# Three short token tiles at the end of each expert layer

## The chip, the cores and the metric

The kernel runs on one core of one Trainium2 chip. The time is device microseconds of one execution; a result is the median over runs. All transfers between HBM and the core's memory go over 16 DMA engines. Engines are named as in the profile: PE is TensorE (PEld its weight loads), DVE is VectorE, ACT is ScalarE, POOL is GpSimd, SP is SyncE. A name with a q behind it (SPq, ACTq) is that engine's queue issuing a transfer.

## The reference

A small vision network on 16 images of 32 x 32 positions with 96 channels, float32: 16,384 tokens. Two blocks follow each other. Each has a mixer over the image (the first with attention along rows and columns, the second a convolution and a state-space scan) and then a layer of experts, each part added to its input:

```python
x = x + mixer0(ln_c(x))
t = t + experts0(ln_t(t))      # t: x as 16384 tokens of 96
x = x + mixer1(ln_c(x))
t = t + experts1(ln_t(t))

def experts(x, gate_w, gate_b, w1, b1, w2, b2):
    scores = einsum('bsd,de->bse', x, gate_w) + gate_b
    probs = softmax(scores)                      # 4 experts
    masked = probs * (probs is among the top 2)
    masked = masked / (sum(masked) + 1e-9)
    h = gelu(einsum('bsd,edh->ebsh', x, w1) + b1)      # 96 -> 384
    y = einsum('ebsh,ehd->ebsd', h, w2) + b2           # 384 -> 96
    return einsum('bse,ebsd->bsd', masked, y)
```

## The kernel before

The program is written by hand, engine by engine: each engine has its own instruction order, and semaphores join them. Nothing is reordered by a scheduler. The stages follow each other: mixer 0, expert layer 0, mixer 1, expert layer 1.

**Routing.** A token goes to a pair of the 4 experts, so there are `NPAIR` = 6 lists. At the end of a mixer each token's row (`ROW` = 104 numbers: 96 values, two gate weights, mean, 1/deviation, token number) is written by GpSimd's indirect DMAs (L585 in layer 0, L699 in layer 1) into its pair's region of the tensor `rows`. Then VectorE runs `planned` (from L1693): from the six counts it works out how many tiles of 512 each list has, and for each of the 37 tile places where its rows start and which two experts it needs. SyncE reads the plan: `pads` (from L481) writes 512 empty rows behind each list (L486), waits for all row scatters, and then loads tile by tile (`tokens`, L502). The number of places is fixed, `TILES` = 37, what the worst split of 16,384 tokens over six lists needs. With the reference's inputs the lists fill 34 places in layer 0 and 35 in layer 1; the places that are left, the last ones, run on empty rows, with every instruction that a full tile has, and the scatter of an empty row writes nothing, since its token number lies outside.

**One tile.** `CPT` = 6 steps c = 0 to 5, three hidden chunks of 128 for each of the two experts. A float32 product is three matmuls (`product`, L1069 to L1071) over rounded high parts and low rests. In step c of tile t:

- TensorE: `up` (3 matmuls, 128 hidden units by 512 tokens into a PSUM bank), then `down` of four steps earlier (`LAG` = 4; 3 matmuls, 96 by 512), in step 2 the transposes of the next tile's tokens (L1081), in steps 2 and 5 the transposes `y_rows` of a finished expert's output (L1109).
- ScalarE: GELU twice (L841 rounded, L842 full), in step 3 the copy of the next tile's tokens, in step 1 the bias of the first expert's output (L808). In steps 2 and 5 it asks for the weights of the next tile (L818): 673 KB for one expert, into one of two buffers, after the output of tile t-1 that used the buffer.
- VectorE: the low rest of the hidden values (L1878) in steps 0, 1, 3, 4; the bias of the second expert (L1849); `combine` (L1857), four additions for each expert; and the normalised tokens of tile t+2 (L1838).
- GpSimd: the low rest in steps 2 and 5 (L605, `ON_POOL`), and behind each of these two of the four scatters of tile t-2 (L596): each is an indirect DMA of 128 rows into the layer's output. Behind the last tile stand the scatters that are left.

A `down` waits for the low rest of its chunk, a GELU for the low rest of three steps before (`HIDS` = 3).

**Between the stages.** After expert layer 0 SyncE waits for all scatters and loads the new `x` (L546). VectorE goes on, behind its last `combine`, with the preparation of mixer 1's weights (L1265 to L1607) and then the first statistics (L1422). After layer 1 the kernel ends with the last scatters.

## Time and profile before

| | us |
|---|---|
| runs shown | 2108.26, 2111.30, 2111.42 |
| median | 2111.3 |
| the profiled execution, own time | 2104.41 |
| its span, first to last instruction | 2102.4 |
| TensorE busy | 1792.5 (85%) |
| VectorE busy | 1574.6 (75%) |
| GpSimd busy | 1288.6 (61%) |
| ScalarE busy | 1127.7 (54%) |
| DMA, mean over the span | 83 GB/s |

Expert layer 0 lies at about 369 to 745 us, expert layer 1 at about 1726 us to the end. A row of a timeline has the start, the duration, the engine, the line of the program, the operation, output<-input, the count, and in brackets how long the engine was idle before it and what released it. Matmuls are pipelined, so two that follow each other overlap in the rows; the time of one is read from start to start. The granted clock (PEclk) is TensorE's, as a share of full speed.

### The profile page before, as it was taken

What the parts mean: (1) busy time and instruction counts of PE and PEld (TensorE: products, weight loads), DVE (VectorE), ACT (ScalarE), POOL (GpSimd) and SP (SyncE); (2) the same over time, 40 slices, a digit from 0 to 9 for tenths busy, and PEclk for the clock granted to TensorE, in tenths of its full rate; (3) what the DMA queues carried; (4) which work ended last, traced back from release to release, by engine and by line L of the source; (5) the groups of instructions that cost most, each with busy time, mean ns of one, the idle gap of its engine ahead of it and who ended that gap; (6) DMA issues with size and microseconds to landing.
All of it is one profiled execution on the core that took longest, in us unless ns stands there. A gap on an engine that the chain in (4) does not pass through costs nothing.

```text
span 2102.4 us, 65544 instructions
## 1 busy us (share of the span) xinstructions
PE 1792.5 (85%) x25858; PEld 1433.2 (68%) x25858; DVE 1574.6 (75%) x5089; ACT 1127.7 (54%) x2201; POOL 1288.6 (61%) x1350
## 2 busy tenths in 40 slices
PE   4877830899999939999999999999999809999997
PEld 2766630677777737887777777777878607777775
DVE  6688761677777657888989898988888737777775
ACT  2434200677777745555555545545544207777775
POOL 3347757378877734545466756556666565776776
PEclk9776665899999969999999999998999559999998
DMA  9310103465555470000000000000000034555553
GB/s 150 90 58 30 33 31 139 134 198 184 183 193 187 141 121 3 3 3 3 4 10 12 11 10 12 9 11 10 12 11 12 16 129 143 189 184 189 184 189 98
DMA packets 95797, 174.94 MB, mean 83 GB/s; under 512 B 53618, under 2 KB 66955, under 8 KB 95492
## 3 DMA queue, kind: packets, MB, share of 16 engines
q10 hardware_dynamic: 21312, 102.00, 14.6%
q1 hardware_dynamic: 56516, 42.48, 8.8%
q0 software_dynamic: 17664, 26.27, 3.7%
q8 instruction: 206, 3.38, 0.7%
q14 instruction: 99, 0.81, 0.1%
HBM read 135.33 MB, written 37.31 MB: 82 GB/s over the span
## 4 chain that ended last, share of the span: by engine, by line
PE 56%; DVE 22%; issue 8%; POOL 6%; ACT 5%; DMA 2%; SPq 0%; DVEq 0%; ACTq 0%; POOLq 0%
PE ps L1069 10%; PE ps L1070 9%; PE ps L1071 9%; PE ps L1150 6%; POOL rows L585 4%; PE ps L1185 3%; PE ps L1199 2%; PE ps L1109 2%; PE ps L1037 2%; ACT rounded L862 2%; PE ps L1081 2%; PE ps L1221 1%; DMA rounded<-weights_by_expert 1%; PE ps L1196 1%; PE ps L1040 1%
## 5 line engine op out<-in xcount | busy, mean ns | idle before, releaser
L1069 PE MATMUL ps<-rounded 97*128 97x512 f32 (+2 forms) x952 | 394.5, 414 | 4.2 <-DVE rounded L1843 2.8
L1070 PE MATMUL ps<-rounded 97*128 97x512 f32 (+2 forms) x952 | 377.2, 396 | 0.0
L1071 PE MATMUL ps<-rounded 97*128 97x512 f32 (+2 forms) x952 | 377.0, 396 | 0.0
L841 ACT ACTIVATE rounded<-ps 128x512 fp32r<-128x512 f32 x444 | 267.3, 602 | 162.1 <-PE ps L1071 157.3
L1150 PE MATMUL ps<-rounded 128*128 128x224 f32 (+1 forms) x2256 | 350.1, 298 | 4.4 <-ACT rounded L862 4.4
L1150 PEld LDWEIGHTS ps<-rounded 128*128 128x128 f32 x2256 | 305.0, 199 | 38.6 <-issue 9.1
L1878 DVE TENSOR_TENSOR rounded<-arena,rounded 128x512 fp32r<-128x512 f32 x296 | 221.8, 750 | 136.2 <-ACT arena L842 135.9
L605 POOL TENSOR_TENSOR rounded<-arena,rounded 128x512 fp32r<-128x512 f32 x148 | 192.5, 1300 | 160.5 <-ACT arena L842 155.7
L842 ACT ACTIVATE arena<-ps 128x512 f32<-128x512 f32 x444 | 267.6, 603 | 0.0
L671 POOL TENSOR_TENSOR w<-arena,consts 128x384 f32<-128x384 f32 x128 | 107.5, 840 | 219.5 <-DVE arena L1361 219.5
L1069 PEld LDWEIGHTS ps<-rounded 97*128 97x128 f32 (+2 forms) x952 | 167.2, 176 | 57.4 <-issue 10.7
L1071 PEld LDWEIGHTS ps<-rounded 97*128 97x128 f32 (+2 forms) x952 | 166.9, 175 | 55.2
L1070 PEld LDWEIGHTS ps<-rounded 97*128 97x128 f32 (+2 forms) x952 | 169.4, 178 | 43.3
L1857 DVE SCALAR_TENSOR_TENSOR arena<-ps,arena 128x96 f32<-128x96 f32 x592 | 146.4, 309 | 60.9 <-PE ps L1109 60.6
L585 POOL DMA_INDIRECT rows<-residual,arena x128 | 131.5, 1028 | 87.5 <-DVEq L1792 49.8
L596 POOL DMA_INDIRECT after_ffn<-arena x148 | 162.8, 1100 | 35.7 <-issue 31.1
L596 POOL DMA_INDIRECT out<-arena x148 | 156.2, 1055 | 35.7 <-issue 29.6
L862 ACT CAST rounded<-rounded 96x992 fp32r<-96x992 f32 (+2 forms) x192 | 155.6, 810 | 6.6 <-DVE rounded L1365 3.9
L699 POOL DMA_INDIRECT rows<-residual,w x128 | 128.7, 1005 | 32.3 <-issue 29.0
L1199 PEld LDWEIGHTS ps<-arena 32*32 32x32 f32 x12288 | 135.1, 107 | 12.9 <-issue 2.0
L1199 PE MATMUL ps<-arena 32*32 32x16 f32 x12288 | 132.5, 181 | 1.6 <-issue 1.2
L1838 DVE TENSOR_SCALAR arena<-arena 128x96 f32<-128x96 f32 x296 | 79.2, 333 | 66.7 <-DMA arena<-rows 47.8
(318 smaller groups left out, 3799.8 us busy)
## 6 DMA issues: line engine op xcount, KB each, us to landing
rounded<-weights_by_expert ACTq DMA_DIRECT2D x148, 673.0 KB, 4.5
arena<-rows SPq DMA_DIRECT2D x74, 208.0 KB, 2.6
residual<-in_x SPq DMA_DIRECT2D x16, 384.0 KB, 7.3
weights_by_expert<-rounded SPq DMA_DIRECT2D x8, 672.0 KB, 3.8
residual<-after_ffn SPq DMA_DIRECT2D x12, 384.0 KB, 6.8
after_ffn<-arena POOLq DMA_INDIRECT x148
out<-arena POOLq DMA_INDIRECT x148
w<-in_w SPq DMA_DIRECT2D x4, 576.0 KB
```

The source lines that it names most:

```text
L585: pool.indirect_dma_start(rows, bass.IndirectOffsetOnAxis(ap=slot[:, g, h:h + 1], axis=0), held_rows[:, g, h, :], None).then_inc(r_out[g % ...
L596: pool.indirect_dma_start(to, bass.IndirectOffsetOnAxis(ap=mine[:, COL_ID:COL_ID + 1].bitcast(U32), axis=0), mine[:, 0:D], None, bounds_ch ...
L605: pool.tensor_tensor(hidr[:, 1, c, :], hid[:, step % HIDS, :], hidr[:, 0, c, :].bitcast(F32), ALU.subtract).then_inc(f["low_pool"], 1)
L841: act.activation(hidr[:, 0, c, :], bank(UPS[step % len(UPS)]), ACT.Gelu)
L842: act.activation(hid[:, step % HIDS, :], bank(UPS[step % len(UPS)]), ACT.Gelu).then_inc(f["gelu"], 1)
L862: return act.copy(dst[:, :, :, to], src[:, :, :, frm].bitcast(F32))
L1069: pe.matmul(dst, left[0], right[0], start=start, stop=False)
L1070: pe.matmul(dst, left[1], right[0], start=False, stop=False)
L1071: return pe.matmul(dst, left[0], right[1], start=False, stop=stop)
L1150: pe.matmul(dst[:, 0:w], x3[:, x_part, n, slot, tokens], wtap[:, w_part, n, y + 1, 0:w], start=(y == 0 and n == x_part == w_part == 0), st ...
L1199: ins = pe.matmul(bank(5)[pb, n * HD:(n + 1) * HD], mm[pb, i % 2, n, :], xdt[pb, c % 2, j, n, :], start=True, stop=True)
L1878: dve.tensor_tensor(hidr[:, 1, c, :], hid[:, step % HIDS, :], hidr[:, 0, c, :].bitcast(F32), ALU.subtract).then_inc(f["low"], 1)
```

## The change

Of the 37 places of a layer the first 34 (`FULL`) stay tiles of 512 tokens and the last 3 (`HALVES`) become tiles of 256. `blocks(t)` and `width(t)` give a place its number of 128-row blocks and its columns; all instructions of a tile take their width from them. A list whose last tile holds at most 256 tokens counts as short; the first three such last tiles go to the short places, and a short place that none claims reads empty rows. Any split of 16,384 tokens over six lists fits into 34 and 3. The plan has 13 more VectorE instructions for this. The number of places, the weights loaded for each and the order of the engines' steps are as before.

```diff
-TILES = (TOK + NPAIR * (T512 - 1)) // T512
+HALVES = 3
+FULL = 34
+TILES = FULL + HALVES
...
+        def blocks(t):
+            return Q if t < FULL else Q // 2
+        def width(t):
+            return blocks(t) * P
...
-                    sp_.dma_start(xs[:, t % XRING, :, :], rows[bass.ds(n, T512), :]...
+                    sp_.dma_start(xs[:, t % XRING, 0:blocks(t), :], rows[bass.ds(n, width(t)), :]...
...
-                def scatter(t, blocks):
+                def scatter(t, some):
...
-                    for i in blocks:
+                    for i in some:
+                        if i >= blocks(t):
+                            continue
...
-                        pool.tensor_tensor(hidr[:, 1, c, :], hid[:, step % HIDS, :], hidr[:, 0, c, :].bitcast(F32), ALU.subtract).then_inc(f["low_pool"], 1)
+                        pool.tensor_tensor(hidr[:, 1, c, 0:width(t)], hid[:, step % HIDS, 0:width(t)], hidr[:, 0, c, 0:width(t)].bitcast(F32), ALU.subtract).then_inc(f["low_pool"], 1)
...
-                        act.activation(hid[:, step % HIDS, :], bank(UPS[step % len(UPS)]), ACT.Gelu).then_inc(f["gelu"], 1)
+                        act.activation(hid[:, step % HIDS, 0:width(t)], bank(UPS[step % len(UPS)])[:, 0:width(t)], ACT.Gelu).then_inc(f["gelu"], 1)
...
-                    product(bank(2 + e)[0:D, :], halves(w[:, :, n, :]), halves(hidr[:, :, c, :]), n == 0, n == CPE - 1).then_inc(f["down"], 1)
+                    product(bank(2 + e)[0:D, 0:width(t)], halves(w[:, :, n, :]), halves(hidr[:, :, c, 0:width(t)]), n == 0, n == CPE - 1).then_inc(f["down"], 1)
...
-                    for i in range(Q):
+                    for i in range(blocks(t)):
...
                 ch.link(dve.tensor_reduce(n_tiles, over[:, :, :], AX.X, ALU.add))
+                ch.link(dve.scalar_tensor_tensor(short_by, n_tiles, -float(T512), count_f, ALU.mult, ALU.add))
+                ch.link(dve.tensor_scalar(short, short_by, -float(T512 // 2), None, ALU.is_le))
+                ch.link(dve.tensor_tensor_scan(short_no, rc["ones"], short, 0.0, ALU.mult, ALU.add))
...
+                ch.link(dve.tensor_reduce(plan_f[:, :, FULL:TILES], half_parts[:, :, :, :], AX.X, ALU.add))
+                ch.done(dve.tensor_scalar(plan_f[:, 0, FULL:TILES], plan_f[:, 0, FULL:TILES], float(SPARE), None, ALU.add))
```

GpSimd at the end of layer 1, before: L605 is the subtraction of a step, L596 the scatters behind it; the last row holds two scatters of tile 34 and four each of 35 and 36.

```order
L605 TENSOR_TENSOR rounded<-arena,rounded 128x512
L596 DMA out<-arena 16384x96 x2
L605 TENSOR_TENSOR rounded<-arena,rounded 128x512
L596 DMA out<-arena 16384x96 x10
L100 UNCONDITIONAL_BRANCH
```

The same in the change (its lines are L627 and L618), from step 5 of tile 33:

```order
L627 TENSOR_TENSOR rounded<-arena,rounded 128x512
L618 DMA out<-arena 16384x96 x2
L627 TENSOR_TENSOR rounded<-arena,rounded 128x256
L618 DMA out<-arena 16384x96 x2
...
L627 TENSOR_TENSOR rounded<-arena,rounded 128x256
L618 DMA out<-arena 16384x96 x4
L103 UNCONDITIONAL_BRANCH
```

Six subtractions are half as wide, the two scatters behind each are still there up to step 2 of tile 36, and behind the last subtraction stand four in place of ten.

TensorE at the start of tile 34 in the change: the last transposes of an output in tile 33, then `up` of tile 34 (128 rows) and `down` of tile 33 (96 rows).

```order
L1131 MATMUL ps<-consts,arena 128x96 x4
L1091 MATMUL ps<-rounded 128x256
L1092 MATMUL ps<-rounded 128x256
L1093 MATMUL ps<-rounded 128x256
L1091 MATMUL ps<-rounded 96x512
L1092 MATMUL ps<-rounded 96x512
```

Before, the same place reads:

```order
L1109 MATMUL ps<-consts,arena 128x96 x4
L1069 MATMUL ps<-rounded 128x512
L1070 MATMUL ps<-rounded 128x512
L1071 MATMUL ps<-rounded 128x512
L1069 MATMUL ps<-rounded 96x512
```

The order is the same; the widths of `up` fall with tile 34, those of `down` four steps later.

## Rows read from the trace of the kernel before

**Rows 1.** Busy table by stretch: us, then busy us (count) per engine, clock, DMA.
```profile
core 0: us, PE busy (x) PEld busy (x) DVE busy (x) ACT busy (x) POOL busy (x), PEclk, DMA share, GB/s
...
1748.00:2080.00 332.00, 331.61 (x1672) 256.53 (x1671) 243.72 (x626) 255.44 (x488) 233.73 (x206) 1.00 0.57 184
...
2074.59:2083.94 9.35, 9.35 (x47) 7.08 (x46) 5.89 (x15) 7.80 (x15) 7.36 (x7) 1.00 0.30 89
2083.94:2089.40 5.46, 3.36 (x19) 2.14 (x17) 3.38 (x13) 0.69 (x1) 4.38 (x5) 0.95 0.03 7
```

**Rows 2.** Timeline of GpSimd, end of layer 1: start, duration, engine, line.
```profile
2056.65 1.28 POOL L605 TENSOR_TENSOR rounded<-arena,rounded 128x512 fp32r<-128x512 f32 x1 [1.76 <-ACT arena L842]
...
2060.64 1.32 POOL L605 TENSOR_TENSOR rounded<-arena,rounded 128x512 fp32r<-128x512 f32 x1
...
2063.43 0.97 POOL L596 DMA_INDIRECT out<-arena  x1 [0.30 <-issue]
...
2083.94 1.31 POOL L605 TENSOR_TENSOR rounded<-arena,rounded 128x512 fp32r<-128x512 f32 x1
2085.42 0.99 POOL L596 DMA_INDIRECT out<-arena  x1 [0.17 <-issue]
...
2096.92 0.97 POOL L596 DMA_INDIRECT out<-arena  x1 [0.30 <-issue]
```

**Rows 3.** Timeline of VectorE, its last piece of layer 1.
```profile
2088.38 0.99 DVE L1857 SCALAR_TENSOR_TENSOR arena<-ps,arena 128x96 f32<-128x96 f32 x4 [0.64 <-PE ps L1109]
```

**Rows 4.** Timeline of TensorE: 512 columns in layer 1, 224 in mixer 1.
```profile
2058.69 0.40 PE L1071 MATMUL ps<-rounded 97*128 97x512 f32 x1
2058.93 0.40 PE L1069 MATMUL ps<-rounded 128*96 128x512 f32 x1
...
1206.40 0.82 PE L1150 MATMUL ps<-rounded 128*128 128x224 f32 x6
```

**Rows 5.** Groups by shape: count, then busy us, mean ns, idle before.
```profile
L842 ACT ACTIVATE arena<-ps 128x512 f32<-128x512 f32 x207 | 124.8, 603 | 0.0
L886 ACT ACTIVATE arena<-ps 128x224 f32<-128x224 f32 x121 | 42.6, 352 | 122.8 <-PE ps L1153 122.4
L683 POOL TENSOR_TENSOR arena<-arena 128x192 f32<-128x192 f32 x128 | 66.2, 517 | 90.1 <-DVE arena L1311 83.7 <-DVE arena L1309 5.2
```

**Rows 6.** The requests for expert weights: one in tile 34, and all landings.
```profile
2058.82 0.34 ACTq L818 DMA_DIRECT2D rounded<-weights_by_expert  x1
...
DMA to landing us min/median/max: 3.9/4.5/6.9
```

**Rows 7.** Timeline and transfers at the end of layer 0.
```profile
702.44 1.28 POOL L605 TENSOR_TENSOR rounded<-arena,rounded 128x512 fp32r<-128x512 f32 x1 [1.75 <-ACT arena L842]
...
729.76 1.32 POOL L605 TENSOR_TENSOR rounded<-arena,rounded 128x512 fp32r<-128x512 f32 x1
...
734.20 0.99 DVE L1857 SCALAR_TENSOR_TENSOR arena<-ps,arena 128x96 f32<-128x96 f32 x4 [0.65 <-PE ps L1109]
...
745.32 34.85 SPq L546 DMA_DIRECT2D residual<-after_ffn  x28
...
752.78 0.74 DVE L1422 BATCH_NORM_STATS2 stats<-residual 128x6 f32<-128x96 f32 x4
...
residual<-after_ffn SPq DMA_DIRECT2D x16, 96.0 KB, 2.4
```

**Rows 8.** Timeline before layer 1: plan, padding, row scatter, tile load; padding's landing.
```profile
1703.37 0.17 DVE L1699 TENSOR_TENSOR_SCAN arena<-xn,arena 128x6 f32<-128x6 f32 x1
...
1707.94 6.12 SPq L486 DMA_DIRECT2D rows<-xn  x6
...
1722.86 0.95 POOL L699 DMA_INDIRECT rows<-residual,w  x1 [0.30 <-issue]
1725.90 5.15 SPq L502 DMA_DIRECT2D arena<-rows  x5
...
rows<-xn SPq DMA_DIRECT2D x6, 208.0 KB, 8.2
```

**Rows 9.** Timeline of TensorE at the start of mixer 1, at the lower clock.
```profile
770.76 1.47 PE L1150 MATMUL ps<-rounded 128*128 128x224 f32 x6
```

More of the change, by code:

```diff
@@ L56 @@
 UNITS = G * SIDE // UNIT
-for n, w in (("onward", P), ("every", P), ("reset", NPAIR * SIDE), ("reset_unit", NPAIR * UNIT), ("k512", SIDE + 1), ("j", TILES), ("j512", TILES), ("step_a", NPAIR), ("step_b", NPAIR),
+for n, w in (("onward", P), ("every", P), ("reset", NPAIR * SIDE), ("reset_unit", NPAIR * UNIT), ("k512", SIDE + 1), ("j", FULL), ("j512", FULL), ("half_no", HALVES), ("origin_spare", NPAIR), ("pair_a", NPAIR), ("pair_b", NPAIR), ("step_a", NPAIR), ("step_b", NPAIR),
              ("origin", NPAIR), ("ones", NPAIR)):
@@ L226, in metaformer @@
         count_f = part(NPAIR)
-        past = part(TILES, NPAIR)
-        picked_ = part(TILES, NPAIR)
+        past = part(FULL, NPAIR)
+        picked_ = part(FULL, NPAIR)
         jump = part(NPAIR)
+        short_by = part(NPAIR)
+        short = part(NPAIR)
+        short_no = part(NPAIR)
+        of_half = part(HALVES, NPAIR)
+        of_pair = part(3, NPAIR)
+        half_parts = part(3, HALVES, NPAIR)
         plan_f = part(3, TILES)
@@ L334, in bank, with scattered @@
             return ps[:, b:b + n, :].rearrange("p a b -> p (a b)")
+        def blocks(t):
+            return Q if t < FULL else Q // 2
+        def width(t):
+            return blocks(t) * P
+        def scattered(l, t):
+            mine = range(t % XRING, TILES, XRING)
+            return 16 * (l * sum(blocks(x) for x in mine) + sum(blocks(x) for x in mine if x <= t))
         def uses(l, t, ring):
@@ L512, in expert_tiles @@
                 for n in range(XRING):
-                    sp_.wait_ge(y_out[n], 16 * Q * uses(l, max(range(n, TILES, XRING)), XRING))
+                    sp_.wait_ge(y_out[n], scattered(l, TILES - 1 - (TILES - 1 - n) % XRING))
             def mixer_weights():
@@ L655, in _ @@
             for n in range(XRING):
-                pool.wait_ge(y_out[n], 16 * Q * uses(0, max(range(n, TILES, XRING)), XRING))
+                pool.wait_ge(y_out[n], scattered(0, TILES - 1 - (TILES - 1 - n) % XRING))
             edges = rounded[:, :, 0:PARTS[2]].rearrange("p s (a w) -> p s a w", w=SIDE).bitcast(F32)
@@ L1107, in y_rows @@
                     need(pe, f["comb"], l * 2 * TILES + 2 * t + e - 1)
-                    for i in range(Q):
+                    for i in range(blocks(t)):
                         ins = pe.transpose(bank(6 + e)[:, i * D:(i + 1) * D], yte[0:D, e, i * P:(i + 1) * P], ident[0:D, 0:D])
@@ L1697, in planned @@
                                           rc["k512"].unsqueeze(1).to_broadcast([P, NPAIR, SIDE + 1]), ALU.is_gt))
+                for n, name in enumerate(("pair_a", "pair_b")):
+                    ch.done(dve.tensor_copy(of_pair[:, n + 1, :], rc[name]))
                 ch.link(dve.tensor_reduce(n_tiles, over[:, :, :], AX.X, ALU.add))
+                ch.link(dve.scalar_tensor_tensor(short_by, n_tiles, -float(T512), count_f, ALU.mult, ALU.add))
+                ch.link(dve.tensor_scalar(short, short_by, -float(T512 // 2), None, ALU.is_le))
@@ new lines, in planned @@
+                ch.link(dve.tensor_tensor_scan(short_no, rc["ones"], short, 0.0, ALU.mult, ALU.add))
+                ch.done(dve.tensor_tensor(of_half[:, :, :], short_no.unsqueeze(1).to_broadcast([P, HALVES, NPAIR]), rc["half_no"].unsqueeze(2).to_broadcast([P, HALVES, NPAIR]), ALU.is_equal))
+                ch.link(dve.scalar_tensor_tensor(short_by, short_no, float(HALVES), short, ALU.is_le, ALU.mult))
+                ch.link(dve.tensor_tensor(n_tiles, n_tiles, short_by, ALU.subtract))
+                ch.done(dve.tensor_tensor(of_half[:, :, :], of_half[:, :, :], short.unsqueeze(1).to_broadcast([P, HALVES, NPAIR]), ALU.mult))
@@ L1708, in planned @@
+                    ch.link(dve.tensor_reduce(plan_f[:, n, 0:FULL], picked_[:, :, :], AX.X, ALU.add))
+                ch.done(dve.tensor_tensor(plan_f[:, 0, 0:FULL], plan_f[:, 0, 0:FULL], rc["j512"], ALU.add))
+                ch.link(dve.tensor_scalar(plan_f[:, 2, 0:FULL], plan_f[:, 2, 0:FULL], 1.0, None, ALU.add))
                 ch.link(dve.tensor_copy(plan[:, :, :], plan_f[:, :, :]))
@@ L1835, in normal_rows @@
                     need(dve, f["xt_pe"], l * TILES + t - 1)
-                    for i in range(Q):
+                    for i in range(blocks(t)):
                         mine = xs[:, t % XRING, i, :]
@@ L1854, in combine @@
                     need(dve, f["comb"], n)
-                    for i in range(Q):
+                    for i in range(blocks(t)):
                         mine = xs[:, t % XRING, i, :]
```

37 lines of the change are left out of this document (19 added, 18 removed).

## The prediction

> **What bounds the kernel now.** I read the busy table by stretch first. In the steady part of an expert layer TensorE is busy 331.61 of 332 us at its full clock (2.4 GHz) [rows 1]: one tile of 512 tokens takes it about 9.5 us, and nobody else is that full. So a tile is worth 9.5 us as long as TensorE is the one that ends last. The timeline of the layer's end tells another story. Every tile gives GpSimd two subtractions (L605) and four scatters (L596). With two scatters behind it a subtraction ends in the next one after 3.99 us (2056.65 to 2060.64) or 3.76 us (2060.64 to the end of the second scatter, 2063.43 + 0.97); so GpSimd needs 7.75 us of the 9.5 and waits for the rest, 1.76 us before the row at 2056.65. Its last subtraction, of (36,5), ends at 2085.25, and then ten scatters follow without a gap, one per 1.275 us, until 2097.89 [rows 2]. VectorE, which feeds them, is done at 2089.37 [rows 3]. **The last 8.5 us before the final landing are GpSimd's alone.** Whoever shortens only TensorE's tiles at the end of a layer meets GpSimd first.
>
> **The change, part by part.** (t,c) is tile t, hidden chunk c; I take the end of layer 1, where the times are from, and carry it over to layer 0.
>
> *TensorE.* Three tiles of each layer have 256 columns. Matmuls of 512 columns start 0.23 to 0.24 us apart (2058.69, 2058.93). There is no 256-column one before, but six of 224 columns take 0.83 us with the last one's 0.28, so (0.83 - 0.28) / 5 = 0.11 us apart [rows 4]. Between these two points 256 columns cost 0.11 + 32 x 0.12 / 288 = 0.124 us. A short tile has 36 of them, 4.5 us, and half the transposes, some 0.6 us: 5.1 to 5.3 us against 9.5. If TensorE stayed the bound, each layer would save 3 x 4.2 = 12.6 us. The 224-column rows were loaded with 128-column weights before each matmul and still came every 0.11 us, so the load was under the matmul before it. The Trainium skill (TensorE: Matmul & The Clock Gate, section The mechanism) says that a weight load overlaps a running matmul only where the row group differs, and (section LDWEIGHTS) gives a load as its columns / 1.2 GHz. By that, an estimate, a 256-column matmul with its load would take 0.21 us and a short tile 8.1 us; the row's 0.11 us speaks against it, and the sum goes by the row.
>
> *ScalarE and VectorE.* The GELU passes over 224 columns take 0.352 us against 0.603 us for 512 [rows 5], so about 0.38 us for 256. Twelve of them, issued overlapped, and the rest of ScalarE's tile stay under 6 us. Both engines stay under GpSimd, below; I cost them at nothing, covered by it.
>
> *GpSimd.* The subtraction is 1.29 us for 512 columns [rows 2], 0.517 us for 192 in a comparable form [rows 5]; linear between them gives 0.67 us for 256, and half of 1.29 with a fixed part of 0.17 gives 0.73. I take 0.73, since it is this operation; the ends are 0.52 (it is no cheaper than 192 columns) and 0.85. A scatter costs the same for any rows. **But the scatters lag two tiles**: while tiles 34 and 35 run short, GpSimd still scatters 32 and 33, four each. So from (33,5) on its chain is: 3.99 us unchanged; then (34,2), (34,5), (35,2), (35,5), (36,2), each a short subtraction and two scatters, 0.57 us less than now: 3 x 3.19 + 2 x 3.42 = 16.4 us; then (36,5), 0.73 us. Its last subtraction ends 21.1 us after 2056.65, at 2077.8, and not at 2085.25: **7.5 us earlier**. Behind it stand four scatters (two of tile 35, two of 36), 4.9 us, in place of ten, 12.6 us: **7.7 us more**. The last combination of VectorE is in time for them: three short matmuls 0.5, the bias 0.45, transposes 0.35 and two additions 0.5, with the handovers 2.0 us after the subtraction, and tile 36's scatters start at 2.7. Layer 1 gains 7.5 + 7.7 = **15.2 us**.
>
> Does GpSimd really end last in between? Three steps of TensorE are 2.2 to 2.7 us, under 3.2. The other candidate is the expert weights: those for tile t+1 are asked for four steps ahead of use, by ScalarE behind its wait for tile t-1's output, and land 4.5 us (3.9 to 6.9) later [rows 6]. Four full steps are 5.7 us, four steps at GpSimd's pace 4.4 us. So weights come late by fractions of a microsecond. Followed through: tile 33's last product ends about 2060.5, its bias output 0.74 us later, the request takes 0.7; asked for at 2062.0, the weights of (35,3) land at 2066.5, TensorE reaches (35,5) at 2068, the GELUs end at 2069.6, GpSimd is free for it at 2070.4. The slack is 0.75 us there, and about 1 us at (36,5). GpSimd is the bound, narrowly.
>
> *Layer 0.* There the next stage does not start with the last scatter but with VectorE: after its last combination (734.20 + 0.99 = 735.19) it prepares the mixer's weights without a gap to 752.78, when the first statistics run. The residual's loads go out from 745.32, right after the last scatter, and a quarter's land 2.4 us after issue [rows 7], so with four issues they have some 4 us to spare and the scatter tail is hidden. Layer 0 gains the 7.5 us of the chain (702.44 to 731.08 is the same stretch as above), and VectorE's own tail: 735.19 - 731.08 = 4.1 us becomes 2.0. **9.6 us**. The load comes 15.2 us earlier and has then 9 us to spare.
>
> *The plan.* 13 small VectorE instructions join each plan. Such a one lasts 0.17 us, so 2.2 us, with 0.03 us of handover each 2.6. Behind the plan are queued: SyncE's six padding writes and ScalarE's first weights. In layer 1 the padding is issued from 1707.94 to 1714.06 and lands 8.2 us later, at 1722.3; with 2.6 us added 1724.9. The tile loads start at 1725.90 because GpSimd's row scatters, the last at 1722.86, have to land [rows 8]. So the plan costs **nothing**, with 1 us to spare; if that cover were gone, 2.6 us. In layer 0 the plan is made some 40 us ahead of the first tile load. Below nothing there is no reason.
>
> *Sum.* 15.2 + 9.6 = 24.8 us. The profiled execution took 2104.4 us (span 2102.4), which becomes 2079.6. The median of the runs shown is 6.9 us above it; I subtract from the median: 2111.3 - 24.8 = **2086.5 us**, 1.2% less.
>
> **Rivals.**
> (a) *GpSimd's part is cheaper.* At 0.52 us a subtraction six of them give 1.3 us a layer, and the first scatter behind each at 0.99 in place of 1.26 us 0.5: 28.4 us in all, 2083. For it: TensorE's limit lies far below. Against it: the weights' slack is 0.75 us.
> (b) *The weights bound the short tiles.* At the largest landing of this trace, 6.9 us, 2.4 - 0.75 = 1.65 us is lost in tile 35 and again in 36, 3.3 us a layer: 18 us gained, 2093.
> (c) *TensorE's clock falls.* It is now busy all the time; in short tiles it works some 5.2 of 6.6 us. After real pauses the clock was at its lower level (1.2 GHz): 0.95 is the mean where work stops [rows 1]; at the lower level six matmuls of 224 columns took 1.47 us [rows 9], (1.47 - 0.43) / 5 = 0.21 us apart, so 0.235 for 256, and a tile 9.1 us. Then the tiles themselves save only 0.4 us each: layer 1 gains 1.2 + 0.6 + 7.7 = 9.5 us, layer 0 1.2 + 0.6 + 1.7 = 3.5; 13 us, 2098. If it falls for the last tile alone, 2090. Against it: the gaps would be of half a microsecond each, not of several.
> (d) *Slower than before.* One mechanism: the weights of tiles 35 and 36 land so late that they eat the gain, 12.4 us a layer on average, in two tiles. That takes 6.2 us + 0.75 us of slack in each, a landing of 11.5 us; above it the kernel is slower, at 14 us by 2 x 2 x 2.5 = 10 us, 2121. For it: they are asked for in shorter steps, while scatters go on. Against it: the largest landing was 6.9 us, and two loads per 6.6 us are only 1.4 times the present rate.
> (e) *The short tiles save nothing*, since tiles that hold padding were cheap already. Against it: every place runs the same instructions, and the rows of 35 and 36 are as long as the others [rows 1]: 9.35 us. That would be 2111.
>
> **How the numbers follow.** My forecast (GpSimd's chain, 2084 to 2090) 0.63; (a) 0.10; (b) 0.13; (c) 0.09; (d) 0.03; (e) 0.02. The range reaches from (a) with 2 us for the runs' own spread to (b) with the milder part of (c): 2081 to 2097; outside are the full (c), (d), (e) and a little of each end, under 2 in 10. About 0.2%, 4 us, is what a measurement of this kernel can tell from no change: faster 0.94, within it 0.03, slower 0.03.
>
> **What would show it.** In the timeline after: six subtractions a layer of 0.65 to 0.8 us, GpSimd without idle from (34,2) to the end, and four scatters behind the last subtraction. A short tile of 6.4 to 6.8 us, TensorE 75 to 85% busy in it at a granted clock of 1.00. In layer 0 the stretch from the last combination to the first statistics stays at 17.6 us. The first tile load still follows the last row scatter by 3 us. If GpSimd shows idle waiting for ScalarE in tiles 35 and 36, and TensorE waits for weights, it is (b); if the clock reads below 0.9 there, (c). I am wrong if short matmuls come slower than 0.15 us apart at full clock, or if the mixer's start does not move with VectorE's tail.

## The result, and the profile after

The changed kernel takes 2087.86 us (median of 4 runs, 2086.30 to 2089.02) against 2111.36 us for the kernel before on the same chip: ratio 0.9884, 95% interval 0.9864 to 0.9903. The medians differ by 23.5 us; forecast were 24.8 us and 2086.5 us. The profiled execution took 2087.0 us (span 2085.0) against 2104.4 (span 2102.4) for that of before. These two spans differ by only 17.4 us, since mixer 1 (first statistics to last row scatter) took 972.3 us in the changed kernel and 970.1 us before, and 3.3 us more had gone in it before the subtraction of (33,5) in layer 0. Such differences come and go from execution to execution (964 to 972 us for mixer 1 over the six kernels run on this chip, none of which touches it), so all that follows is read from local stretches, not from spans.

GpSimd at the end of layer 1, timeline of the changed kernel (start, duration, engine, line, operation, output<-input, idle before); it answers to [rows 2]:

```profile
2053.65 1.28 POOL L627 TENSOR_TENSOR rounded<-arena,rounded 128x512 fp32r<-128x512 f32 x1 [1.60 <-ACT arena L864]
...
2057.37 0.75 POOL L627 TENSOR_TENSOR rounded<-arena,rounded 128x256 fp32r<-128x256 f32 x1
2058.29 1.21 POOL L618 DMA_INDIRECT out<-arena  x1 [0.17 <-PE ps L1093]
2059.81 1.00 POOL L618 DMA_INDIRECT out<-arena  x1 [0.31 <-issue]
2061.22 0.73 POOL L627 TENSOR_TENSOR rounded<-arena,rounded 128x256 fp32r<-128x256 f32 x1 [0.41 <-ACT arena L864]
...
2068.13 0.73 POOL L627 TENSOR_TENSOR rounded<-arena,rounded 128x256 fp32r<-128x256 f32 x1 [0.42 <-ACT arena L864]
...
2074.63 0.74 POOL L627 TENSOR_TENSOR rounded<-arena,rounded 128x256 fp32r<-128x256 f32 x1
2075.54 0.99 POOL L618 DMA_INDIRECT out<-arena  x1 [0.17 <-issue]
2076.84 0.97 POOL L618 DMA_INDIRECT out<-arena  x1 [0.30 <-issue]
2078.73 0.97 POOL L618 DMA_INDIRECT out<-arena  x1 [0.92 <-issue]
2080.00 0.97 POOL L618 DMA_INDIRECT out<-arena  x1 [0.30 <-issue]
```

From the subtraction of (33,5), the first row, to the end of that of (36,5) it is 2075.37 - 2053.65 = 21.7 us, before 28.6. Four scatters stand behind it and end 5.6 us later, at 2080.97, where ten took 12.6. Together 27.3 us in place of 41.2: **13.9 us** less. The third of the four is the first scatter of tile 36, and the kernel lets it wait for VectorE's last combination, which ends at 2077.56. This row names no releaser for its gap of 0.92 us; the same row in layer 0 of the run small_weights (below) names VectorE. Before, VectorE was done 8.5 us ahead of the last scatter [rows 3]:

```profile
2077.02 0.54 DVE L1892 SCALAR_TENSOR_TENSOR arena<-ps,arena 128x96 f32<-128x96 f32 x2 [0.48 <-PE ps L1131]
```

TensorE in a short tile of layer 0, timeline; it answers to [rows 4]:

```profile
716.00 0.38 PE L1091 MATMUL ps<-rounded 97*128 97x256 f32 x1 [0.76 <-DMA rounded<-weights_by_expert]
716.22 0.28 PE L1092 MATMUL ps<-rounded 97*128 97x256 f32 x1
716.34 0.28 PE L1093 MATMUL ps<-rounded 97*128 97x256 f32 x1
716.45 0.28 PE L1091 MATMUL ps<-rounded 128*96 128x256 f32 x1
716.57 0.28 PE L1092 MATMUL ps<-rounded 128*96 128x256 f32 x1
```

Matmuls of 256 columns start 0.12 us apart. The busy table by stretch shows TensorE at its full clock in the short tiles, and no longer full (columns: stretch and its length, then busy us and count of PE, PEld, DVE, ACT, POOL, then clock, DMA share, GB/s); it answers to [rows 1]:

```profile
2045.00:2055.00 10.00, 10.00 (x55) 7.93 (x54) 7.13 (x17) 7.76 (x18) 7.39 (x7) 1.00 0.58 182
2055.00:2065.00 10.00, 7.92 (x62) 7.12 (x61) 6.15 (x20) 5.78 (x20) 8.23 (x9) 1.00 0.66 208
2065.00:2075.00 10.00, 8.10 (x66) 7.41 (x64) 5.02 (x15) 6.12 (x20) 8.16 (x10) 1.00 0.35 112
```

What TensorE waited for between 2052 and 2080 us, from the view of waits (us in total, times, longest):

```profile
PE ps L1091 <- DMA rounded<-weights_by_expert: 4.0, 3, 1.9
PE ps L1131 <- DVE arena L1884: 0.6, 1, 0.6
PE ps L1091 <- POOL rounded L627: 0.2, 1, 0.2
```

In layer 0 the last combination ends 23.6 us after the subtraction of (33,5) starts, before 32.75: 9.1 us less. Behind it stands something that was not forecast. The stretch to the first statistics is 19.14 us, before 17.59 [rows 7]. The timeline of that stretch, VectorE and GpSimd, has it in two rows:

```profile
735.33 1.49 DVE L447 CAST rounded<-arena 96x192 fp32r<-96x192 f32 x1
735.33 1.37 POOL L685 MEMSET rounded<- 2x1536 f32 x1
```

A cast that took 0.26 us before takes 1.49 us, and it starts with the last of the memsets by which GpSimd prepares the mixer (three lines, L683 to L685). That is 1.23 of the 1.55 us. Most of the rest lies just ahead of it: an operation on 2x224 numbers takes 0.63 us in place of 0.28, beside the first of these memsets:

```profile
734.50 0.63 DVE L1294 TENSOR_SCALAR arena<-arena 2x224 f32<-2x224 f32 x1
733.78 1.22 POOL L683 MEMSET rounded<- 128x288 f32 x2 [1.32 <-issue]
```

Before, GpSimd came to its memsets at 745.23, after ten scatters, 4.5 us after the start of this cast:

```profile
740.77 0.26 DVE L427 CAST rounded<-arena 96x192 fp32r<-96x192 f32 x1
...
747.37 2.00 POOL L663 MEMSET rounded<- 2x1536 f32 x1
```

The sum by local stretches: 13.9 + 9.1 - 1.5 = 21.5 us. The interval of the ratio stands for 20.5 to 28.7 us, so it holds this sum as well as the forecast.

### The profile page after: what moved, and what is told of

It reads as the page before. It is cut to its first block, busy times and chain, and to the rows that moved or that the text cites. A ratio compares the mean times of both kernels' runs of the same rounds, so it can differ in the third digit from the quotient of the medians.

```text
span 2085.0 us, 65444 instructions
## 1 busy us (share of the span) xinstructions
PE 1779.2 (85%) x25822; PEld 1430.2 (69%) x25822; DVE 1561.8 (75%) x5079; ACT 1110.3 (53%) x2201; POOL 1267.4 (61%) x1338
## 4 chain that ended last, share of the span: by engine, by line
PE 57%; DVE 21%; issue 8%; POOL 5%; ACT 5%; DMA 3%; SPq 1%; ACTq 0%; DVEq 0%; POOLq 0%
PE ps L1091 10%; PE ps L1092 9%; PE ps L1093 9%; PE ps L1172 7%; PE ps L1207 3%; POOL rows L605 3%; PE ps L1221 3%; PE ps L1131 2%; ACT rounded L884 2%; DMA rounded<-weights_by_expert 2%; PE ps L1046 2%; PE ps L1243 2%; PE ps L1059 2%; PE ps L1218 1%; PE ps L1103 1%
## 5 line engine op out<-in xcount | busy, mean ns | idle before, releaser
L1091 PE MATMUL ps<-rounded 97*128 97x512 f32 (+4 forms) x952 | 386.9, 406 | 13.7 <-DMA rounded<-weights_by_expert 6.9
L1092 PE MATMUL ps<-rounded 97*128 97x512 f32 (+4 forms) x952 | 369.4, 388 | 0.0
L1093 PE MATMUL ps<-rounded 97*128 97x512 f32 (+4 forms) x952 | 368.7, 387 | 0.0
L863 ACT ACTIVATE rounded<-ps 128x512 fp32r<-128x512 f32 (+1 forms) x444 | 259.8, 585 | 167.0 <-PE ps L1093 160.4
L1913 DVE TENSOR_TENSOR rounded<-arena,rounded 128x512 fp32r<-128x512 f32 (+1 forms) x296 | 216.3, 731 | 142.0 <-ACT arena L864 141.9
L627 POOL TENSOR_TENSOR rounded<-arena,rounded 128x512 fp32r<-128x512 f32 (+1 forms) x148 | 185.7, 1255 | 157.0 <-ACT arena L864 154.2
L864 ACT ACTIVATE arena<-ps 128x512 f32<-128x512 f32 (+1 forms) x444 | 260.2, 586 | 0.0
L605 POOL DMA_INDIRECT rows<-residual,arena x128 | 131.5, 1027 | 84.4 <-DVEq L1827 46.7
L1892 DVE SCALAR_TENSOR_TENSOR arena<-ps,arena 128x96 f32<-128x96 f32 x568 | 141.1, 310 | 54.9 <-PE ps L1131 54.6
L618 POOL DMA_INDIRECT after_ffn<-arena x142 | 155.2, 1093 | 34.1 <-issue 29.4
L618 POOL DMA_INDIRECT out<-arena x142 | 149.3, 1051 | 34.5 <-issue 28.5
L1207 PE MATMUL ps<-w,consts 128*128 128x384 f32 x256 | 127.1, 581 | 0.0
```

The costliest lines, as they stand in the source:

```text
L605: pool.indirect_dma_start(rows, bass.IndirectOffsetOnAxis(ap=slot[:, g, h:h + 1], axis=0), held_rows[:, g, h, :], None).then_inc(r_out[g % ...
L618: pool.indirect_dma_start(to, bass.IndirectOffsetOnAxis(ap=mine[:, COL_ID:COL_ID + 1].bitcast(U32), axis=0), mine[:, 0:D], None, bounds_ch ...
L863: act.activation(hidr[:, 0, c, 0:width(t)], bank(UPS[step % len(UPS)])[:, 0:width(t)], ACT.Gelu)
L864: act.activation(hid[:, step % HIDS, 0:width(t)], bank(UPS[step % len(UPS)])[:, 0:width(t)], ACT.Gelu).then_inc(f["gelu"], 1)
L1091: pe.matmul(dst, left[0], right[0], start=start, stop=False)
L1092: pe.matmul(dst, left[1], right[0], start=False, stop=False)
```

## The experiments

All local stretches are measured from a GpSimd subtraction, to the end of VectorE's last combination (the end of layer 0, as far as the mixer is concerned) or to the end of the last scatter (the end of layer 1).

| kernel | (33,5) to last combination, layer 0 | (33,5) to last scatter, layer 1 | (29,5) to the same, layers 0 / 1 | ratio to before, 95% interval |
|---|---|---|---|---|
| before | 32.75 | 41.24 | 71.07 / 79.20 | |
| the change | 23.61 | 27.32 | 61.41 / 64.89 | 0.9884 (0.9864 to 0.9903) |
| plan_only | 32.94 | 41.24 | 71.54 / 78.99 | 0.9983 (0.9952 to 1.0013) |
| narrow_rows_only | 30.64 | 34.18 | 68.81 / 71.71 | 0.9938 (0.9913 to 0.9963) |
| four_scatters | 23.72 | 33.97 | 61.76 / 71.51 | 0.9893 (0.9861 to 0.9924) |
| small_weights | 23.75 | 26.80 | 61.56 / 64.35 | 0.9878 (0.9847 to 0.9908) |
| wide_subtraction | 26.44 | 29.91 | 64.24 / 67.46 | 0.9924 (0.9868 to 0.9980) |
| vector_subtracts | 25.84 | 29.39 | 63.70 / 66.91 | 0.9877 (0.9830 to 0.9925) |
| spread | - | - | 60.42 / 65.91 | 0.9827 (0.9785 to 0.9870) |
| late_memsets | 24.00 | 26.92 | 61.84 / 64.43 | one execution, 2212.07 us |
| change_again | 25.11 | 27.21 | 63.13 / 64.74 | 0.9875 (0.9834 to 0.9915) |
| spread_again | - | - | 59.89 / 66.09 | 0.9907 (0.9876 to 0.9939) |
| memsets_last | 24.55 | 27.29 | 62.34 / 64.90 | 0.9890 (0.9842 to 0.9937) |
| last_on_vector | 25.16 | 27.09 | 62.97 / 64.62 | 0.9905 (0.9871 to 0.9939) |

From wide_subtraction on the runs are from other chip time, in which the kernel before took 2207.6 and 2211.2 us in the median, 4.6 to 4.8% more than beside the first runs (2109.5). The steady part of the expert layers is as long there (37.5 us for four tiles of layer 1 in both); what is longer is the rest, for one the step from the last row scatter to the first tile load, 9.3 to 10.2 us in place of 3.05, and mixer 1, 997 to 1028 us. Ratios compare with before on the same chip; from the single execution of late_memsets only rows are read.

### The plan alone

Short places keep tiles of 512; the plan of the change stays.

```diff
         def blocks(t):
-            return Q if t < FULL else Q // 2
+            return Q
```

> The new plan alone: the last three places run 512 wide again, with four scatters each, and read the rows behind their short lists as empty ones. If the plan's 13 instructions are hidden under the row scatters, the time is that of the kernel before, 2111 us (within 3), and the first tile load of each layer still starts 3.0 us after the last row scatter. If the plan is on the path: 2 to 5 us above, and that distance grows by as much.

Nothing moved: both ends are those of before within 0.2 us, the first tile load follows the last row scatter by 3.06 us (before 3.04), and 17.60 us lie between last combination and first statistics. With four scatters in every tile GpSimd's memsets come late again and cast L447 takes 0.26 us, so the 1.5 us belong to the early end of GpSimd and not to the plan.

### Half the rows, full width

Tiles 34 to 36 load, add and scatter two blocks, but compute all 512 columns.

```diff
         def width(t):
-            return blocks(t) * P
+            return T512
...
-                    sp_.dma_start(xs[:, t % XRING, 0:blocks(t), :], rows[bass.ds(n, width(t)), :]...
+                    sp_.dma_start(xs[:, t % XRING, 0:blocks(t), :], rows[bass.ds(n, blocks(t) * P), :]...
```

> The last three places load, normalise, add and scatter two blocks, but TensorE's products, the GELUs and the low rests stay 512 wide. What is gained is the scatter tail alone. GpSimd's chain: in layer 1 four scatters behind the last subtraction in place of ten, held back by the last addition (about 3.7 us after the subtraction), so 6.3 us gained; in layer 0, where VectorE sets the end, 0.5 us. Together 7 us below the kernel before, 2104. If GpSimd's scatters were not what ends layer 1, it would be within 1 us of it.

Layer 1 ends 7.1 us earlier than before, 6.3 of them in the tail behind the last subtraction (6.32 us in place of 12.64) and 0.7 in the chain ahead of it. Half of what layer 1 gained is thus the number of scatters alone, whatever the tiles compute. Layer 0 gains 2.1 us at the last combination, where 0.5 were expected, and gives 1.5 us back: here too the memset starts with the cast and it takes 1.49 us.

### Half the width, four scatters

```diff
                     for i in some:
-                        if i >= blocks(t):
-                            continue
```

with the count of scatters that the waits expect raised to match.

> The change with four scatters again in the short tiles (the two added ones write once more the rows that their buffer still holds from six tiles before). GpSimd's chain up to the last subtraction is the same, behind it stand ten scatters in place of four: +7.7 us in layer 1, nothing in layer 0 (the residual's loads have over 8 us to spare): 7.7 above the change, 2095.5. If the scatter tail of layer 0 counted as well: 15 above.

The mirror image. The last combination comes as in the change (23.72 us); the last scatter of layer 1 ends 6.65 us later, with ten scatters 1.275 us apart behind the last subtraction. The median misses the expectation: 2086.95 us, where 2095.5 was expected. It doesn't show the 6.65 us, though its interval (to 0.9924) just has room for them, and in the profiled execution mixer 1 was 5.6 us shorter. I take the local stretch; the ratio alone would leave it open. Taken together the two halves give the whole: 7.1 us by rows, and 13.9 - 6.65 = 7.3 us by width.

### Weights that take no time

For tiles 35 and 36 only the last 66 columns of the weights are loaded, 34 of 673 KB each; their results are not the experts' for these tiles.

```diff
+                    some = slice(0, WROW) if t <= FULL else slice(WROW - 66, WROW)
-                    act.dma_start(wring[:, t % 2, e, :]..., wsp[l, bass.ds(n, 1), :, :]...
+                    act.dma_start(wring[:, t % 2, e, some]..., wsp[l, bass.ds(n, 1), :, some]...
```

> The change, with only the last 66 columns (34 of 673 KB) of the expert weights loaded for tiles 35 and 36 of each layer; the rest of the buffer keeps the weights of two tiles before, so these tiles compute with other weights. If GpSimd's chain is the bound and the weights come late under its cover: at most 1.5 us below the change, 2086.5, and GpSimd's subtractions of (34,5) to (36,5) follow the scatters ahead of them without idle. If the weights bound the short tiles: some 6 us below, 2082, and the short tiles take 5.5 us in place of 6.6.

TensorE's waits from 2052 to 2080 us, as above for the change:

```profile
PE ps L1092 <- POOL rounded L627: 1.9, 2, 1.6
PE ps L1132 <- DVE arena L1885: 1.8, 3, 1.0
```

The 4.0 us of waiting for weights are gone, and TensorE waits for GpSimd's subtraction instead. GpSimd's last subtraction ends 0.4 us earlier in layer 0 (21.0 after 21.4 us) and 0.7 us earlier in layer 1 (21.0 after 21.7), the last combination of layer 0 no earlier at all, and the last scatter of layer 1 0.5 us earlier. Between the last subtraction and the last combination this run loses something of its own, 2.7 us in layer 0 and 2.4 in layer 1 in place of 2.2: TensorE's granted clock fell to 0.50 there, behind its wait of 1.6 us for GpSimd. VectorE is waited for in layer 0:

```profile
728.40 0.48 DVE L1885 TENSOR_SCALAR arena<-ps,rounded 96x256 f32<-96x256 f32 x1 [2.05 <-PE ps L1094]
730.94 0.97 POOL L618 DMA_INDIRECT after_ffn<-arena  x1 [1.15 <-DVE arena L1893]
```

**Weights cost the change 0.4 and 0.7 us in GpSimd's chain**, though TensorE is seen waiting for them for 4.0 us in layer 1. The line of a wait says what came last, not what it costs.

### Subtractions as wide as before

```diff
-                        pool.tensor_tensor(hidr[:, 1, c, 0:width(t)], hid[:, step % HIDS, 0:width(t)], ...
+                        pool.tensor_tensor(hidr[:, 1, c, :], hid[:, step % HIDS, :], ...
```

> The change, with GpSimd's subtraction 512 wide again in the short tiles (the added columns hold leftovers and are read by nobody); every other width is that of the change. If GpSimd's chain sets the short tiles: six times 0.55 us, the stretch from the subtraction of (33,5) to the end of the last one grows from 21.4 and 21.7 us by 3.0 to 3.4 us in each layer, in all some 6.5 us above the change. If the weights or TensorE set them: under 1 us a layer.

The last combination comes 2.8 us later in layer 0 and the last scatter 2.6 us later in layer 1, against the change's first profile; six subtractions were 6 x 0.55 = 3.3 us longer, so 0.5 to 0.7 us went into what had been idle. The chain up to the last subtraction grew by 2.8 and 2.6 us, a little under the 3.0 to 3.4 expected. GpSimd's chain sets the end of both layers nearly one for one. TensorE's clock was at 0.50 for 3.4 us in each layer of this run, and GpSimd, never idle for more than 0.42 us between its subtractions, covered it.

### All short subtractions on VectorE

The two subtractions a tile that GpSimd does are done by VectorE (0.43 us each) in tiles 34 to 36.

```diff
+        def on_pool(t, c):
+            return c in ON_POOL and t not in (34, 35, 36)
...
-                    if c in ON_POOL and step < LAST:
+                    if step < LAST and on_pool(t, c):
...
-                    if step < LAST and c not in ON_POOL:
+                    if step < LAST and not on_pool(t, c):
```

> The change, with the six subtractions of the short tiles given to VectorE, which is busy 60% there: GpSimd only scatters. GpSimd's chain would be 4.5 us a layer shorter; then the weights, which came late by 0.4 to 1.9 us at three places under its cover, are next. I expect 2 to 3 us a layer, some 5 us below the change, with TensorE's waits for weights growing. If GpSimd were not the bound: no gain.

This expectation missed, and by its sign: both layers end 2.1 to 2.2 us **later** than in the change's first profile (0.7 and 2.2 us later than in change_again, below, whose layer 0 had a lower clock too). GpSimd is out of the way (it waits up to 3.68 us for combinations in layer 0), and what stands in its place is TensorE. Timeline of TensorE in tile 35 of layer 0, and the busy table of that stretch:

```profile
767.40 0.38 PE L1097 MATMUL ps<-rounded 97*128 97x256 f32 x1 [1.59 <-ACT arena L870]
...
769.35 0.58 PE L1136 MATMUL ps<-consts,arena 96*128 96x96 f32 x2 [0.76 <-ACT arena L837]
...
770.42 0.41 PE L1097 MATMUL ps<-rounded 128*96 128x256 f32 x1
770.63 0.41 PE L1098 MATMUL ps<-rounded 128*96 128x256 f32 x1
```

```profile
764.00:767.00 3.00, 1.67 (x12) 1.46 (x12) 0.37 (x2) 0.31 (x2) 2.23 (x3) 1.00 0.69 208
767.00:770.00 3.00, 1.84 (x12) 1.59 (x13) 1.88 (x7) 1.90 (x7) 0.00 (x0) 0.76 0.19 73
770.00:773.00 3.00, 3.00 (x16) 3.00 (x16) 2.13 (x7) 2.13 (x7) 2.39 (x3) 0.50 0.64 185
773.00:776.00 3.00, 3.00 (x17) 2.73 (x17) 1.47 (x6) 1.50 (x5) 1.88 (x2) 0.60 0.63 184
```

Behind the wait of 1.59 us, and as the one of 0.76 us begins, its granted clock falls: it is 0.50, that is 1.2 GHz, from 768.6 to 775.4, and its matmuls start 0.21 us apart in place of 0.12. The 24 matmuls with 256 columns of that time cost 24 x 0.095 = 2.3 us more. In layer 1 the clock reads 0.78 from 2180 to 2183 and 0.65 from 2183 to 2186, and TensorE also waited 2.2 us for ScalarE's output evacuation (L837). Why ScalarE came late in both layers I could not tell from the rows. Shown is that no microsecond was to be had by freeing GpSimd in this way; that it would be without the fall of the clock is not shown.

### Short tiles apart from each other

Places 30, 34 and 36 are the short ones, so that full tiles lie between.

```diff
+SHORT = [30, 34, 36]
...
-            return Q if t < FULL else Q // 2
+            return Q // 2 if t in SHORT else Q
```

> The three short places at 30, 34 and 36 in place of 34, 35 and 36. Between short tiles stand full ones, in which GpSimd has 1.7 us to spare, so its lag is worked off and TensorE's 4.2 us a short tile are gained almost in full: 12.6 us in the tiles, less up to 1 us for weights each time. Behind the last subtraction of layer 1 stand six scatters (four of tile 35, two of 36): 5 us less than before the change. Layer 0 gains 3 to 5 us over the change, layer 1 1 to 4: 4 to 8 us below it, 2080 to 2084. If GpSimd's lag were not what eats the short tiles' gain, this would be 2.5 us slower than the change, for the two scatters.

> The short tiles at the places 30, 34 and 36. By the local stretches of its first run (60.4 us to the last combination of layer 0, 65.9 us to the last scatter of layer 1, against 61.4 and 64.9 us for the change) it is even with the change: within 2 us, ratio 0.985 to 0.990. If its ratio of 0.983 was its own, it is 10 us below the change on the same chip. I expect even.

The first ratio, 0.983, looked like another 0.5%; it did not come back. With the change itself run beside it on the same chip, spread_again has 0.9907 and change_again 0.9875, their intervals overlapping. The local stretches say the same: 1.0 to 1.5 us earlier at the last combination of layer 0 than the change's first profile, 1.0 to 1.2 us later at the last scatter of layer 1, since tile 35 has four scatters again and six stand behind the last subtraction, for 7.6 us:

```profile
2180.23 0.75 POOL L631 TENSOR_TENSOR rounded<-arena,rounded 128x256 fp32r<-128x256 f32 x1
2181.24 0.99 POOL L622 DMA_INDIRECT out<-arena  x1 [0.27 <-issue]
...
2187.64 0.97 POOL L622 DMA_INDIRECT out<-arena  x1 [0.30 <-issue]
```

The 4 to 8 us that were expected are not there, and no gain over the change is shown. One thing sets these two runs apart from the others of this chip time: from tile 29 on TensorE's granted clock reads 1.00 to the last combination in both layers, and its longest wait there is 0.6 us.

### The memsets and the cast

late_memsets lets GpSimd wait ahead of its memsets until VectorE comes to the end of its splits; memsets_last moves that point behind the casts that follow.

```diff
+            pool.wait_ge(split_done, 1)
             edges = rounded[:, :, 0:PARTS[2]]...
...
                 ch.link(split(dve, ch, by_row[:, :, 2, 0:CONV], wright[0:D]))
+                dve.sem_inc(split_done, 1)
```

> The change, with GpSimd's three memsets after layer 0 held back until VectorE has split the mixer's weights. In the change VectorE's first split there, a 96x192 cast, took 1.49 us in place of 0.26, while GpSimd's 2x1536 memset ran. If the two get in each other's way, the stretch from VectorE's last addition to the first statistics goes back from 19.1 to 17.6 us; if the cast is slow for another reason it stays.

> The change, with GpSimd's three memsets ahead of the mixer waiting until VectorE has done its last large cast. Theory (memset and cast hold one another up): all casts are short as in the kernel before, the stretch from the last combination to the first statistics is 17.6 us in place of 19.1 us, and the time 1.5 us lower. Rival (the casts are slow for another reason, or the memsets are wanted at once by ScalarE): the stretch stays at 18.5 to 19.1 us, or what is gained comes back as a wait of ScalarE for the memsets right behind it.

> The change itself, as the reference for the three kernels beside it on this chip. Ratio to the kernel before 0.985 to 0.990. From the start of the subtraction of (29,5) to the end of VectorE's last combination of layer 0: 61.4 us; to the end of the last scatter of layer 1: 64.9 us. Last combination to first statistics: 19.1 us (theory: GpSimd's three memsets run beside VectorE's casts and hold one of them); a rival, that 19.1 was a chance of that one execution, gives 17.6 us.

The stretch from last combination to first statistics, and where the time sits (the memset of 2x1536 is the last of the three lines):

| kernel | stretch, us | memset of 2x1536 starts | cast of 96x192 | casts of 32x1344 |
|---|---|---|---|---|
| before, plan_only | 17.59, 17.60 | late | 0.26 | 1.81, 1.82 |
| the change, change_again | 19.14, 19.19 | with the cast | 1.49, 1.49 | 1.74, 1.74 |
| four_scatters | 18.39 | behind the cast | 0.29 | 2.09 |
| spread, spread_again | 18.40, 18.42 | behind the cast | 0.26, 0.26 | 1.74, 1.74 |
| late_memsets | 18.50 | behind the cast | 0.26 | 2.59 |
| memsets_last | 18.03 | behind the cast | 0.26 | 2.09 |

change_again has the 1.49 us again, so it was no chance. With the gate in place the cast is 0.26 us, as in the kernel before; but the memsets now meet the next casts. In memsets_last:

```profile
785.79 0.26 DVE L448 CAST rounded<-arena 96x192 fp32r<-96x192 f32 x1
...
791.27 2.09 DVE L1621 CAST rounded<-rounded 32x1344 fp32r<-32x1344 f32 x2
...
791.45 2.43 POOL L685 MEMSET rounded<- 128x288 f32 x2 [8.26 <-DVEq L1624]
```

Both are longer than apart (1.74 and 1.23 us). VectorE's instruction that opens the gate (L1624) stands behind these casts, and yet GpSimd was released 0.2 us into them: it does not wait for the casts ahead of it, so the gate opened earlier than the line's place suggests. In four_scatters the same memset, from 741.61, took 2.19 us and met the same casts; in spread the memsets met casts of 96x672 and 96x16 (0.74 and 0.56 us in place of 0.61 and 0.16). So the theory that memset and cast hold one another up is borne out in each of these kernels, at another cast each time; the expected 17.6 us were not reached, 18.03 were. The Trainium skill (SBUF — State Buffer, section SBUF: two separate sides) says why: VectorE and GpSimd share one pair of ports as an exclusive lock for a whole instruction, and the loser blocks. It says this of a VectorE operation in a mode that uses both ports, or one with two inputs in SBUF against a GpSimd operation that reads it. The rows agree: 1.49 us is about the 1.37 us of the memset that had started, plus the rest of the cast, and the memset that began behind a cast took 2.00 us in place of 1.37. Not every cast takes part: in memsets_last the memset of 1.37 us at 794.20 ran beside the three casts of 32x672, which took 2.59 us there as everywhere. Those casts take 0.86 us each, as long as the casts of twice that width (1.74 us for two), so they run at half the rate; that they lack the mode of which the page speaks fits this, but no row names the mode. An operation of 2x224 took 0.53 us in four_scatters in place of 0.28 while GpSimd was issuing scatters and no memset ran; why is open. In time the gate is worth 1.2 us at most, 0.05%; the ratio (0.9890, against 0.9875 for change_again) cannot show it.

### The last tile's subtractions on VectorE

As above, for tile 36 alone.

```diff
+            return c in ON_POOL and t not in (36,)
```

> The change, with the two subtractions of the last tile alone on VectorE (0.43 us each there) in place of GpSimd (0.75 us each). If GpSimd's chain is the bound to the very end: two subtractions fewer on it, 1.3 to 1.5 us earlier at the last combination and the last scatter (60.0 us and 63.5 us from (29,5)). If, as with all three tiles on VectorE, TensorE is then reached by a wait or a lower clock: no gain, or 1 to 2 us worse (62 to 63.5 us and 65 to 67 us).

The second case came: no gain. Both layers end within 0.2 us of change_again. In layer 0 both ran partly at the lower clock, so the reading rests on layer 1. TensorE, layer 1, timeline of change_again and then of last_on_vector; the first row of each is the start of chunk 3 of tile 36, held up by weights, the last the final product:

```profile
2157.38 0.38 PE L1091 MATMUL ps<-rounded 97*128 97x256 f32 x1 [1.43 <-DMA rounded<-weights_by_expert]
...
2162.10 0.36 PE L1091 MATMUL ps<-rounded 128*96 128x256 f32 x1 [0.81 <-POOL rounded L627]
```

```profile
2169.21 0.39 PE L1097 MATMUL ps<-rounded 97*128 97x256 f32 x1 [1.59 <-DMA rounded<-weights_by_expert]
...
2173.49 0.38 PE L1136 MATMUL ps<-consts,arena 96*128 96x96 f32 x2 [0.61 <-ACT arena L837]
...
2173.66 0.34 PE L1097 MATMUL ps<-rounded 128*96 128x256 f32 x1
```

Counted from the subtraction of (33,5) (2140.45 and 2152.02) the weights release TensorE at 16.9 and 17.2 us, and the final product starts at 21.65 and 21.64 us. In change_again it waits 0.81 us for GpSimd; with the subtraction on VectorE that wait is gone, and in its place the product stands behind an output transpose that waits 0.61 us for ScalarE. **In the last tile the two chains, GpSimd's and the one from the weights through TensorE, are level**; taking GpSimd's away gave 0.1 us here, and taking the weights away gave 0.5 us at the end of layer 1 in small_weights.

## Why the prediction held, point by point

- *TensorE, 0.124 us a matmul, full clock.* Measured 0.12 us, at a clock of 1.00 in the profiled execution. (The six matmuls of 224 columns stand with 0.82 us in [rows 4], not 0.83; the spacing is 0.11 either way.) The estimate of 0.21 us from two rules of the Trainium skill (TensorE: Matmul & The Clock Gate, sections The mechanism and LDWEIGHTS (loading the stationary operand)) was wrong here: 0.21 us is what is seen only where the granted clock is 0.50.
- *The subtraction, 0.73 us.* Measured 0.73 to 0.76 us, six a layer. The fixed part of 0.17 us that the forecast took stands in none of its rows; 1.30 us for 512 columns and 0.743 for 256 in the change give 0.19.
- *A short tile of 6.4 to 6.8 us, TensorE 75 to 85% busy.* From (34,5) to (35,5) and on to (36,5) it took 6.9 and 6.5 us in layer 1, 7.0 and 6.4 in layer 0, with TensorE busy 71 to 85%.
- *GpSimd's chain, 21.1 us.* Measured 21.7 us in layer 1 and 21.4 us in layer 0. The step that failed is "GpSimd without idle from (34,2) on": it waits 0.41 and 0.42 us for ScalarE ahead of (34,5) and (35,5), whose GELUs hang on the weights. The slack of 0.75 us that was counted for the weights at (35,5) was not there: TensorE waited 0.6, 1.5 and 1.9 us for weights in the three tiles of layer 1. At (36,5) GpSimd did not wait. Rival (b) came in in this way, at 0.4 and 0.7 us a layer by small_weights and not at 3.3.
- *The scatter tail, 4.9 us in place of 12.6.* Measured 5.6 us. The last combination ends 2.2 us after the last subtraction (forecast 2.0), and tile 36's scatters start at 3.4, not at 2.7: the 0.7 us lie between the combination's end and the scatter (1.2 us, of which 0.92 show as idle of GpSimd). This handover was left out of the sum.
- *Layer 1, 15.2 us.* Measured 13.9: 0.6 of the difference in the chain, 0.7 in the tail.
- *Layer 0, 9.6 us at the last combination.* Measured 9.1: 0.3 of the difference in the chain (7.2 us for 7.5), 0.2 in VectorE's tail (2.2 us, forecast 2.0).
- *"The stretch from the last combination to the first statistics stays at 17.6 us."* Wrong, 19.1 us. The step costed GpSimd's early end at nothing, with the loads of the residual in view and not the three memsets behind the last scatter. [rows 7] has the subtractions, the last combination, the loads and the first statistics, and neither the memsets nor the casts. A step that ends earlier also starts its successor earlier, and that successor can collide with what it used to avoid.
- *The plan, nothing.* Right on this chip: 3.05 us from last row scatter to first tile load in both. In change_again that step is 9.3 us and the last of SyncE's padding writes is issued by 1807.6, behind the last row scatter (1801.6), so the cover of the plan's 2.6 us (an estimate; no run measures it) may be gone there; plan_only was not run there.
- *The sum, 24.8 us.* 21.5 us by local stretches, 23.5 by medians. Forecast mechanism and places were right (GpSimd's chain and its scatters, by wide_subtraction, four_scatters and narrow_rows_only); 1.3, 0.5 and 1.5 us were missed in layer 1, layer 0 and the preparation.
- *Rival (c), the clock.* Not in the first profiled execution. It came in change_again, in layer 0: clock 0.66 from 770 to 773 and 0.77 to 776, behind waits for weights of 3.3 us in two; there the last combination came 25.11 us after (33,5), 1.5 us later than in the first profile. Nor was it alone: in layer 0 the clock fell to 0.50 for 3.4 to 6.8 us in all six kernels of the other chip time whose short tiles stand together (wide_subtraction, vector_subtracts, late_memsets, change_again, memsets_last, last_on_vector), and in layer 1 ahead of the last product in wide_subtraction and vector_subtracts. Where GpSimd's work was the change's own, the last combination of layer 0 came 0.4, 0.9 and 1.5 us later than in the first profile (late_memsets, memsets_last, change_again). That the forecast of 1.00 held in the first profile was thus in part luck. Rivals (a), (d) and (e) did not occur.

```profile
767.00:770.00 3.00, 1.75 (x15) 1.45 (x13) 1.40 (x4) 2.40 (x9) 2.04 (x3) 1.00 0.76 245
770.00:773.00 3.00, 2.24 (x11) 2.24 (x12) 0.65 (x2) 0.72 (x3) 2.52 (x4) 0.66 0.06 14
773.00:776.00 3.00, 3.00 (x23) 2.91 (x22) 1.14 (x4) 2.00 (x6) 1.59 (x2) 0.77 0.02 0
```

No kernel here is shown to beat the change. By rows, memsets_last is ahead of it by 1.2 us in one stretch, and spread by some 1 us in all (layer 0 and the stretch behind it 1.7 to 2.2 us shorter, layer 1 1.0 to 1.2 us longer), both under what a measurement can tell.

## What to carry to other kernels

Work that is cut from the bound engine at the end of a stage is worth what the next-slower chain allows: list for the last tiles what each engine still has queued, scatters of older tiles included, and add the pieces up from a common mark. Ask of each engine that gets done earlier what it starts next and beside whom; here the memsets took back 1.5 of 9 us. And read a wait as a name, not as a price: 4.0 us of waiting for weights were worth 0.7 us in GpSimd's chain and 0.5 at the end of the layer, because another chain stood right behind.

## What the runs showed of the hardware

- Some GpSimd memsets and VectorE casts hold one another up: a cast of 96x192 went from 0.26 to 1.49 us beside a memset of 1.37 us, and such a memset from 1.37 to 2.00 us behind a cast of 32x1344. Casts of 32x672 and a memset of 1.37 us ran beside each other at full speed.
- A semaphore increment of VectorE's own that stands behind a cast does not wait for it: in memsets_last it released GpSimd 0.2 us into five casts that ended 4.5 us later.
- TensorE at a granted clock of 1.00 does a matmul of 256 columns (97x128 or 128x96 weights, loaded before each) every 0.12 us, and every 0.21 us at 0.50. The clock fell in layer 0 of vector_subtracts behind a wait of 1.6 us and of change_again behind waits for weights of 1.3 and 2.0 us. In the change's first profile it stayed at 1.00, in layer 0 with waits of up to 0.9 us, but in layer 1 with waits of 0.6, 1.5 and 1.9 us; so the longest wait alone does not tell when it falls.
- The same program was 4.6 to 4.8% slower in other chip time with its full expert tiles just as fast (37.5 us for four), so a ratio from one place is not safe for a change of another stage.
